# Flamingo cross-attention and routed experts: GpSimd adds three key blocks of the probabilities, and normalising moves from VectorE to ScalarE

## What is computed

```python
q = split_heads(layernorm(x)) * 32 ** -0.5
k, v = split_heads(ctx[..., :512]), split_heads(ctx[..., 512:])
logits = einsum('bhqd,bhkd->bhqk', q, k) + b + mask(length)
x = x + tanh(g_xattn) * merge(einsum('bhqk,bhkd->bhqd', softmax(logits), v))
y = layernorm(x)
logits = y / norm(y) @ (cent / norm(cent)).T + y @ w_route.T
gates = top_2_softmax(logits)                # 8 experts
h = gelu(y @ w1 + b1);  z = h @ w2 + b2      # per expert
x = x + tanh(g_ffn) * sum_e gates_e * z_e
```

## Time and profile before

| what | us |
|---|---|
| median of 3 runs (lowest, highest) | 2121.07 (2115.35, 2128.86) |
| the profiled execution, its own time | 2121.86 |
| its span in the profile | 2119.7 |
| PE busy | 1891.6 (89%) |
| DVE busy | 1565.7 (74%) |
| ACT busy | 1096.3 (52%) |
| POOL busy | 715.6 (34%) |
| mean granted TensorE clock | 0.965 |

### The profile page before, as it was taken

The page is one execution under the profiler, slowest core; times in us unless marked ns, Lnnn a source line. Parts: engine busy times, 40 slices in busy tenths (PEclk is TensorE's granted clock), DMA queues, the critical chain, the costliest instruction groups (busy, mean ns, idle before and its releaser), DMA issues. The chain is left out here.

```text
span 2119.7 us, 38741 instructions
## 1 busy us (share of the span) xinstructions
PE 1891.6 (89%) x10720; PEld 1050.8 (50%) x10721; DVE 1565.7 (74%) x3713; ACT 1096.3 (52%) x1970; POOL 715.6 (34%) x547
## 2 busy tenths in 40 slices
PE   0599999999999999999999999999379899998987
PEld 0344444444444444444444444443257677676765
DVE  6577788777877878877777787874467677766775
ACT  0155555556656555565655656565244444454443
POOL 1112111111111101111111111100068888888887
PEclk9999999999999999999999999999589999999999
DMA  3877677667777777777677686763358786877784
GB/s 110 137 116 154 114 182 143 129 152 122 184 142 130 162 115 182 145 134 160 123 168 145 128 170 123 148 129 106 100 114 148 146 143 130 153 135 134 131 155 69
DMA packets 173114, 292.01 MB, mean 138 GB/s; under 512 B 37982, under 2 KB 42078, under 8 KB 172944
## 3 DMA queue, kind: packets, MB, share of 16 engines
q1 hardware_dynamic: 140016, 222.26, 51.6%
q0 software_dynamic: 32928, 67.68, 18.2%
HBM read 127.09 MB, written 71.63 MB: 94 GB/s over the span
## 5 line engine op out<-in xcount | busy, mean ns | idle before, releaser
L918 DVE TENSOR_REDUCE mx<-bank 128x1 f32<-128x512 f32 x1024 | 692.3, 685 | 239.4 <-PE bank L714 220.8
L622 ACT ACTIVATE prob<-bank 128x512 f32<-128x512 f32 x1024 | 578.5, 595 | 491.8 <-PE bank L702 491.7
L590 POOL TENSOR_TENSOR regrouped_then_w<-regrouped_then_w 128x512 fp32r<-128x512 f32 x128 | 164.8, 1287 | 1145.8 <-ACT regrouped_then_w L612 1145.8
L714 PE MATMUL bank<-stA,stB 98*128 98x512 f32 x1024 | 428.9, 421 | 66.6 <-DVE mx L918 41.7
L702 PE MATMUL bank<-stB,stA 100*128 100x512 f32 x1024 | 469.0, 460 | 8.7 <-issue 8.4
L702 PEld LDWEIGHTS bank<-stB,stA 100*128 100x128 f32 x1024 | 196.8, 193 | 212.1 <-ACT prob L622 113.3
L675 PE MATMUL bank<-prob,vin 128*32 128x512 f32 x2048 | 281.2, 622 | 0.0
L675 PE MATMUL bank<-prob,ones 128*32 128x512 f32 x2048 | 277.8, 615 | 0.0
L1153 POOL DMA_INDIRECT rows_in<-xn_rows,gather_ids x152 | 207.8, 1367 | 162.5 <-DVE rows_in L1363 121.1
L714 PEld LDWEIGHTS bank<-stA,stB 98*128 98x128 f32 x1024 | 202.8, 198 | 113.4 <-DVE mx L918 73.2
L1183 POOL DMA_INDIRECT out_dram<-yout,scatter_ids x144 | 238.1, 1653 | 40.4 <-issue 35.9
(11 more groups left out here) (184 smaller groups left out, 2170.5 us busy)
## 6 DMA issues: line engine op xcount, KB each, us to landing
stB<-regrouped_then_w SPq DMA_DIRECT2D x192, 256.0 KB, 5.7
stA<-regrouped_then_w SPq DMA_DIRECT2D x192, 256.0 KB, 8.3
x_k_then_w<-in_x_dram SPq DMA_DIRECT2D x16, 1024.0 KB, 6.3
x_k_then_w<-in_ctx_dram SPq DMA_DIRECT2D x16, 1024.0 KB, 8.6
vin<-in_ctx_dram SPq DMA_DIRECT2D x16, 1024.0 KB, 6.4
xres<-in_x_dram SPq DMA_DIRECT2D x16, 1024.0 KB, 12.5
xn_rows<-xn SPq DMA_DIRECT2D x64, 256.0 KB, 2.3
out_dram<-xres SPq DMA_DIRECT2D x16, 1024.0 KB, 10.8
```

The source lines that it names most:

```text
L590: pool.tensor_tensor(turnedL[:, side, :], turned[:, side, :], turnedH[:, side, :].bitcast(F32), ALU.subtract).then_inc(s_lo, 1)
L622: act.activation(prob[:, u % 2, j, :], psS[j % 2][:, :], ACT.Exp).then_inc(s_exp, 1)
L714: pe.matmul(psM[s % 2][:, :], stB[0:98, g, j, i * P:(i + 1) * P], stA[0:98, g, j, :], start=True, stop=True).then_inc(s_m, 1)
L918: dve.tensor_reduce(mx[:, s // 4, s % 4:s % 4 + 1], psM[s % 2][:, :], AX.X, ALU.max).then_inc(s_mx, 1)
```

## The change

- **Sums.** `prob` has four blocks. The first two change places from step to step (`prob_of`), the third and fourth stay. POOL adds block 1 to block 0, head by head, and then block 2: eight additions of 128 x 512 a step, the first after the first value product. PE multiplies the sum and block 3 by ones (`sums`, slot 2 of the next step) into a turn bank of its own turn "SM"; ACT copies it (slot 3). An exp block waits for what read its place a step before.
- **Value products** come once in four slots (`values`), V is loaded by group, two steps ahead.
- **Maxima.** The bank of the sums becomes a third bank of the maxima (`max_bank`; `bank_back` says how many maxima back the bank's last one lies).
- **Normalising.** Both normalisations are ACT operations (`Identity` with scale and bias): Q in slots 7, 9, 12 and 14 of the first step of a batch, the row block in slot 8 of each step. DVE makes the shift (-mean x rstd) for them. The multiplication of the sums by tanh goes: the addition to x has it as its scalar (`scalar_tensor_tensor`).
- **K** is regrouped one group at a time on POOL, at the end of each step, behind the additions.
- **Order.** Turns: Q (slot 0), SM (2), K (3), MT (5), DT (7), OT (9), XT (10), LG (14). DVE's chains move: Q's to slots 5 to 12 of the fourth step, two operations a slot, the row's to slots 0 to 8 of the second step, two a slot. Statistics of the next batch move to slots 0 to 4 of the third and fourth steps. SP places the maxima after K's high parts and before its low part; the load of the resident x goes to the end of SP's step. The expert weights load from three steps later, two a step.

```diff
-TURNS = [("TQ", 3), ("XT", -5), ("MT", 1), ("TK", 3), ("DT", -1), ("OT", -1), ("LG", -5)]
+TURNS = [("TQ", 3), ("SM", -1), ("TK", 3), ("MT", 1), ("DT", -1), ("OT", -1), ("XT", -5), ("LG", -5)]
...
-            psS, psM, psT, psO, psD = banks[0:2], banks[2:4], banks[4:6], banks[6], banks[7]
+            psS, psM, psT, psO = banks[0:2], [banks[2], banks[3], banks[7]], banks[4:6], banks[6]
+            max_bank = [s % 3 for s in range(15)] + [1]
+            bank_back = [4, 2, 4] + [3] * 12 + [2]
...
+            def prob_of(st, off, u):
+                return prob[:, u if u >= 2 else (st.l + off + u) % 2, :, :]
...
             @block.gpsimd
...
-                    if st.g() == 0 and st.on(4):
+                    if st.on(0):
+                        first, more, then = [prob_of(st, 0, u) for u in range(3)]
+                        pool.wait_ge(s_pv, st.count(PV, 0, 1))
+                        for j in range(HG):
+                            pool.wait_ge(s_exp, st.count(16, 0, HG + j + 1))
+                            pool.tensor_tensor(first[:, j, :], first[:, j, :], more[:, j, :], ALU.add).then_inc(s_acc, 1)
+                        for j in range(HG):
+                            pool.wait_ge(s_exp, st.count(16, 0, 2 * HG + j + 1))
+                            pool.wait_ge(s_acc, st.count(ADDS, 0, j + 1))
+                            pool.tensor_tensor(first[:, j, :], first[:, j, :], then[:, j, :], ALU.add).then_inc(s_acc, 1)
+                    if st.on(4):
...
-                        pool.tensor_copy(kg[:, :, :].rearrange("p i (g c h) -> p (i g) h c", g=NG, h=HG),
-                                         kin[:, kpar, :, :].rearrange("p i (g h c) -> p (i g) h c", g=NG, h=HG)).then_inc(s_kg, 1)
+                        pool.tensor_copy(kg[:, st.l % 2, :, :].rearrange("p i (c h) -> p i h c", h=HG),
+                                         kin[:, kpar, :, g * P:(g + 1) * P].rearrange("p i (h c) -> p i h c", h=HG)).then_inc(s_kg, 1)
...
             @block.scalar
...
+                    act.activation(xn2[:, half, :], xres[:, par, i, :], ACT.Identity, bias=shift2[:, i:i + 1],
+                                   scale=rsb[:, i:i + 1]).then_inc(s_xn2, 1)
...
             @block.tensor
...
+                def sums(st, off):
+                    pe.wait_ge(s_acc, st.count(ADDS, off, ADDS))
+                    bank, done = put_turn(pe, st, "SM")
+                    for u in (0, NT - 1):
+                        p = prob_of(st, off, u)
+                        for j in range(HG):
+                            last = pe.matmul(bank[DH * j:DH * (j + 1), :], ones[:, 0:DH], p[:, j, :],
+                                             start=(u == 0), stop=(u > 0), skip_group_check=True,
+                                             tile_position=(0, DH * j))
+                    last.then_inc(done, 1)
...
-                                pe.wait_ge(s_mx, st.count(16, 2, s - 1))
-                            pe.matmul(psM[s % 2][:, :], stB[0:98, g, j, i * P:(i + 1) * P], stA[0:98, g, j, :],
+                                pe.wait_ge(s_mx, st.count(16, 2, s + 1 - bank_back[s]))
+                            pe.matmul(psM[max_bank[s]][:, :], stB[0:98, g, j, i * P:(i + 1) * P], stA[0:98, g, j, :],
...
             @block.vector
...
+                        if st.g() == 1 and s <= 8 and st.on(-5):
+                            row_scale(st, 2 * s)
+                        if st.g() == 3 and 5 <= s <= 12 and st.on(5):
+                            scale(st, 2 * (s - 5))
...
+                        if st.g() == 1 and s <= 8 and st.on(-5):
+                            row_scale(st, 2 * s + 1)
+                        if st.g() == 3 and 5 <= s <= 12 and st.on(5):
+                            scale(st, 2 * (s - 5) + 1)
...
-                        if s == 6 and st.on(-1):
...
-                            dve.tensor_scalar(rsum[:, :, :], rsum[:, :, :], tanh_a[:, 0:1], None, ALU.mult).then_inc(s_rsum, 1)
...
-                            dve.tensor_tensor(dst, dst, scaled[:, :, :], ALU.add).then_inc(s_x1a, 1)
+                            dve.scalar_tensor_tensor(out=dst, in0=scaled[:, :, :], scalar=tanh_a[:, 0:1], in1=dst,
+                                                     op0=ALU.mult, op1=ALU.add).then_inc(s_x1a, 1)
```

More of the change, by code:

```diff
@@ L426, in flamingo_kernel @@
             s_kg = sem("k_regrouped")
+            s_acc = sem("probs_added")
             s_full = sem("turned_copied")
@@ L633, in step @@
                             act.activation(mT[:, :], bank[0:2 * HG, :], ACT.Copy).then_inc(took, 1)
-                        if s in (2, 4) and st.on(-1):
-                            name, dst, src, done = ("DT", sumT, psD, 7) if s == 2 else ("OT", attT, psO, 8)
-                            act.wait_ge(s_pv, st.count(8, -1, done))
-                            if st.rnd is not None or st.l - 1 >= 2:
-                                b, before = turn_of(st, name, -2)
-                                act.wait_ge(s_turn[b], before + 1)
-                            act.activation(dst[:, (st.l + 1) % 2, :], src[:, :], ACT.Copy).then_inc(s_out, 1)
+                        if s == 8 and st.on(-5):
+                            normalise(st)
+                        if s == 11 and st.on(-5):
+                            bank, took = take_turn(act, st, "XT")
+                            act.activation(xT[:, :, :].rearrange("p k t -> p (k t)"), bank[:, :], ACT.Copy).then_inc(took, 1)
+                        if st.g() == 0 and s in (7, 9, 12, 14) and st.on(4):
+                            normalise_q(st, (7, 9, 12, 14).index(s))
                         if s == 10 and st.g() == 1 and st.on(-6):
```

329 lines of the change are left out of this document (182 added, 147 removed).

## The result

The changed kernel takes 2304.17 us (median of 4 runs, 2293.73 to 2326.03), against 2122.55 us before in the same session: ratio 1.086, 95% interval 1.083 to 1.090, slower. The forecast had the direction, but it expected 71 us more and 182 came: 2304 lies above its own range (2145 to 2260) and just inside the outer bounds, 2005 to 2310. The execution in the profile is the longest of the four, 2326.03 us, so what is read from it adds up to some 20 us more than the median.

The account below looks back on a forecast made before the run. Attention's steps bound the kernel: PE's 18.5 us, but DVE held by POOL in the second and fourth. A batch goes from 87.4 to 93.0 us; 2121.9 + 78 (fourteen batches) - 8 = 2192 us, range 2145 to 2260.

Parts of the forecast that it names:

- outer bounds: Whole time: low end 2005 us, rival A with its step at 17.5; high end 2310 us, between forecast and Rival C.
- The failed step: DVE, first and third steps: four operations held by POOL, 3.1 us in all; 16.9 and 17.7 us, both below 18.5.
- Rival C: DVE is passed over while POOL has something queued, from slot 11 of every step; 103 a batch, 2332 us; chance 0.13.
- The clock: PE's lower clock beside longer waits costs nothing while DVE sets the pace; only a reason to round up.
- The chains: Second and fourth steps: each POOL operation lets one DVE chain operation through; 9.8 us held, steps 30.4 and 27.3 us.
- PE's own time: PE's step falls from 20.3 to 18.0 us; taken as 18.5, bounds 18.0 and 19.5.
- ACT: First step: Q normalisations moved to ACT at 0.6 us each (0.5 to 1.0); 15.8 us busy, hidden under 18.5.
- DMA: V loads in 64 pieces with 512 B rows could cost some 3 us a batch; taken as nothing, being two steps early.
- The edges: First steps, last batch without a Q chain, and drain give back some 8 us, within 15 either way.
- The chances: Slower 0.61, within 1% 0.08, faster by over 1% 0.31; the forecast itself 0.48.
- rival A: Each POOL operation lets two chain operations through, half the hold: 83.6 a batch, 2061 us, faster; chance 0.22.

Follow-up runs that it names:

- Experiment 12: Changed kernel with one more semaphore wait a step: POOL's fifth addition waits until the fourth is complete; 2173.97 us, ratio 1.022 to the kernel before.
- Experiments 6: Changed kernel with each POOL addition waiting by semaphore for the one before to be complete; 2114.89 us, ratio 0.996 to the kernel before.
- experiment 1: Changed kernel without POOL's eight additions, so the sums are those of blocks 0 and 3 alone; 1995.72 us, ratio 0.938 to the kernel before.
- experiment 2: Changed kernel with the scaled output written back to its PSUM bank, where the addition to x reads it; 2165.29 us, ratio 1.018 to the kernel before.

## Why the prediction was right or wrong

**The failed step** is "In the first and third only the logit, the addition to x and the two of the maxima's negation are held, for half an operation to a whole". The addition to x was held 3.4 us beyond its own time in the first steps and 3.7 in the third (the forecast had 3.1 us for four operations, some 0.8 each), and "16.9 and 17.7, both below 18.5" became 23.0 and 21.8. Experiment 12 removes just the passing over, and with it the low clock behind it, and leaves the rest of the holds: 2174 us and 91.8 a batch. So this one mechanism costs 130 of the 182 us, and without it the gap of 112 us to the forecast (2192) would be gone. That 2174 and 2192, 91.8 and 93.0 lie so close is in part luck: in experiment 12 the first step is 21.3 us (forecast 18.5) and the second 24.7 (30.4), and the two misses cancel.

**Rival C** named it ("passed over as long as POOL has something queued", from slot 11, 22.5 us for the first and third steps) and its steps and sum were the nearest of all: 103 a batch, 2332 us. It was wrong in one thing: it had the addition to x passed over in every step, and in the second and fourth it lasts 1.55 and 0.74 us. I gave it 0.13 because the earlier trace rows showed a chain that was let in. That was right for chains and no evidence for an operation that comes alone into a long row of additions. The forecast treated as one mechanism what the traces show to be two cases. The Trainium skill (GPSIMD Engine Reference, "Instruction dispatch") says that consecutive Pool instructions aren't a barrier between the eight cores, and that an instruction counts as complete for who waits on its semaphore only when all eight are done. Experiments 6 and 12 agree with what this may mean here: after several operations the cores have drifted apart so far that no moment is free of all of them, and a wait or a DVE operation let in brings them together. No run shows the single cores, so drift is argued and not shown; shown is the tendency of the count, and that a wait ends the passing over.

**The clock** "costs PE nothing while DVE sets the pace": wrong, and a second term put at nothing. The low clock behind the waits of the first and third steps reaches into the steps that follow; in the second ones it is 2.5 us of PE's time (experiment 12). PE's work in the third step is 18.27 us at clock 1.00 in experiment 12 and 19.00 at 0.97 in the changed kernel; over sixteen steps it is 339.1 us at 0.88 against 301.5 at 0.98 in experiment 1, for the same 1793 records. Part of this lies under DVE's waits; how much in all does was not separated.

**The chains** were right in the rule (one operation let in by each POOL operation: ten of sixteen in the fourth step) and somewhat high in the price (7.9 us against 9.8; in the second step 7.6 with the masks of the routing, against 12.4), since twelve of the row chain's eighteen operations run in POOL's gap. The second step was 27.8 us, not 30.4. The fourth was 29.0, not 27.3. In the second and fourth steps PE also waits for the inverted sums behind the chain (L819 for L1023, 8 times in sixteen steps, up to 2.7 us), and every second fourth step ends the loop's body and has the wait that nothing names; the forecast had neither.

**PE's own time** was nearly right: 18.3 against 18.0. The double product of the sums takes its 1.93 us (L758 from 842.62), forecast 2.0. **ACT** was undersized: a normalisation of Q has 1308 ns in its row and adds 1.0 us to ACT's busy time ((17.44 - 13.4) / 4), where I took 0.6; ACT is busy 17.4 us in a first step, not 15.8. "Were it 1.0 each, 17.4 is still hidden" is nearly true: without additions PE waits there 0.75 us for ACT. **DMA** at nothing was right: V lands 6.6 us after its issue, two steps ahead of its use, and no wait of PE names it; parts of `stA` land in 5.6 us, sooner than before.

**The edges** were to give back 8 us. They did not: in the profiled executions attention lost 208 us, the twelve batches of the loop 165 of them, and fourteen batches of the same loss would be 192. The edges added some 16 us.

**The chances**: 0.61 for slower was on the right side; the likeliest number was too low, and the case that came nearest had 0.13. The low end of the outer bounds is mis-stated: rival A with its step at 17.5 sums to 81.6 a batch and 2033 us; 2005 is A with every step 1 us shorter.

## What to carry to other kernels

In these kernels a GpSimd addition or copy holds the DVE operations that come while it runs and work elementwise from SBUF to SBUF (tensor_tensor, scalar_tensor_tensor, tensor_scalar, copy), and the length of the hold goes with how long GpSimd has run without a break: after up to two operations the DVE one is nearly always in at the next boundary, after five it mostly waits until GpSimd waits. So it is worth trying a semaphore wait of GpSimd on its own predecessor in a long row of operations (here 0.1 us of pause bought 130 us), dependent DVE chains belong in GpSimd's gaps, and a DVE operation on the critical path may read one input from PSUM instead (742 ns, never held, in experiment 2). And where one fix exposes another wait, as moving the chains did for the addition to x, look at the pair before judging either: alone the chains' move gave 26 us and the PSUM input 139, together 227.

## What the runs showed of the hardware that was not expected

- A DVE operation of 32 numbers per partition lasts 4.24 us, and one of 512 numbers 6.84 us, though three and nine POOL operations ended meanwhile without letting it in.
- Not every DVE operation with its input in SBUF is held: bn_stats of 128 and 512 numbers never lasts over 0.29 and 0.69 us in the changed kernel (150 to 1450 us), as in the kernel before.
- Behind PE's wait for a late maximum the next step begins at a low granted clock: 0.72 in the first 8 us of the second steps on average, 1.00 in experiment 12, where the wait is gone.
- Waiting for its own predecessor makes POOL slower (1.36 us apart instead of 1.24) and the kernel 8% faster.
- Twice as many GpSimd operations of half the size take 0.69 us each from start to start, 1.38 for the pair against 1.24, and the addition to x was passed over for longer beside them (mean 4.5 us against 2.7).
- PE's unexplained wait at the turn of the loop is up to 3.7 us in the changed kernel and 4.3 in experiment 1, against 1.7 before (705 to 1055 us). What it waits for is open.
